# Both ends of an attention stage in new orders, and one turned tile in another PSUM bank

## The chip, the cores and the metric

The kernel runs on one core of one Trainium2 chip. The metric is the device time of one execution in microseconds (us); less is better.

A core has TensorE (PE, matrix products out of SBUF into the accumulators, PSUM), VectorE (DVE), ScalarE (ACT), GpSimd (POOL) and SyncE (SP, which here only issues transfers). Each engine runs its own instructions in the order in which the program lists them, and an instruction that has to wait for another engine holds up all that stand behind it on its own.

## The reference, cut to what matters

A macaron layer: half a feed-forward part, an attention part, half a feed-forward part, each added to its input. Tokens are 1024, channels C = 256, heads 16 of 16 channels, the inner width of the feed-forward part 768.

```python
x = x + 0.5 * ffn(layernorm(x))
x = x + attn(layernorm(x))
x = x + 0.5 * ffn(layernorm(x))

def attn(x):
    q, k, v = split(x @ w_qkv)
    q, k = xpos(q), xpos(k)
    scores = (q @ k.T) * D ** -0.5 * decay_mask
    y = scores @ v
    yn = (y - mean(y)) / sqrt(var(y) + eps)
    yn = yn * gn_weight + gn_bias
    return (silu(x @ w_g) * yn) @ w_proj

def ffn(x):
    return ((silu(x @ Wg * gs) * (x @ Wu * us)) @ Wd) * ds
```

The mean and variance in attn are over the 16 channels of a head. The score mask is causal and decays by a factor of the head for each step of distance.

## The kernel before, in words

**Tiles and stages.** The tokens are cut in NT = 8 tiles (in attention: chunks) of 128. The first feed-forward part works on two groups of four tiles: products gate and up in transposed form (gate_up, line 1148), then down (line 1171), which makes one token tile from 12 products of 128x128 by 128x256: six parts of the inner width, each in a high and a low half. `down(d, first, last)` does the parts from first to last, so a call can be cut in two. Attention runs chunk by chunk as a linear recurrence: a state of 16x16 per head is carried from chunk to chunk, and within a chunk the masked scores are multiplied out. The second feed-forward part follows as the first.

**One chunk c of attention.** PE turns the normalized tile (turn_h2, line 1201), ACT copies it (copy_h2, 465), PE makes q and k (project_qk, 1214), v (project_v, 1226) and the gate (project_g, 1239). DVE rotates q and k in two steps: rotate_parts (779, two products with the rotation table, out of the PSUM bank) and rotate (792, a difference and a sum). PE turns the result (turn_qk, 1254) and makes the scores (1265), DVE masks them in four instructions (mask_scores, 804). y is the sum of state times q (apply_state, 1285) and masked scores times v (values, 1297), in the lower half of PSUM bank 0 (`b_y`); the upper half holds the gate product (`b_g`). The state's new part is update_state (1312) on PE, mask_kv (812) on DVE, add_state (342) on POOL. ACT copies y out (copy_y), PE turns it back to tokens by channels (turn_y, 1323), ACT squares it (gsq) and copies it (gd) in take_y (520), DVE sums the squares per head (group_var, 838), POOL forms (sum/16 + eps) to the power -1/2 (group_roots, 332: a short instruction and the power on line 340), DVE multiplies (group_norm, 844, tile gn), PE turns it again (turn_gn, 1340), ACT applies weight and bias (affine, 530), DVE multiplies by the gate (gated, 852), PE multiplies by w_proj (project_out, 1353), and DVE adds it to the residual (add_proj, 859).

**The norm of a tile.** DVE makes mean and variance (tile_stats, 697, and mean_var, 707), POOL the root (roots, 312: lines 316 and 318), DVE the normalized tile (norm_tile, 718). Tiles are numbered through: 0 to 7 in the first part, 8 to 15 in attention, 16 to 23 in the second. Tiles 16 to 19 are turned by turn_h(2) (1101), eight transposes, and split by ACT and PE for the second feed-forward part.

**What sets the order.** Everything is ordered by hand: for each engine the calls are written out one after the other (POOL from line 350, ACT from 541, DVE from 864, PE from 1364), and each operation waits for counts of semaphores named after what has been done. On DVE the middle chunks are a loop (973 to 987), in front of it stand the instructions of chunks 0 and 1, behind it chunks 5 to 7 by hand. On PE the loop is on lines 1439 to 1452, the front of attention on 1405 to 1438, the back on 1453 to 1483. POOL's back is on lines 385 to 394.

**The banks.** `b_turned_y` and `b_gn` say in which PSUM bank the turned y and the turned gn (and behind it the output product) of each chunk lie: bank 7 for chunks 0 to 6 of the one and 0 to 5 of the other, lower half for y, upper half for gn. turn_y therefore waits for the readers of that bank:

```python
if c == 0:
    pe.wait_ge(yd_done, NT)
elif c == NT - 1:
    pe.wait_ge(sc_masked, HG * NT)
else:
    pe.wait_ge(gd_done, c)
```

Of the kernel before, what the change touches and what calls it, by code (L numbers as in the profile page):

```python
# [32 lines left out]
T, C, I = 1024, 256, 768  # L33
# [94 lines left out]
def macaron(nc, x, w_qkv, w_g, w_proj, gn_w, gn_b, gate_w, up_w, down_w, gate_s, up_s, down_s,  # L128
            rotation_t, mask_t, out):
    with ExitStack() as ctx:  # L130
# [86 lines left out]
        b_v, b_kv = bank[2][:, 0:C], bank[2][:, C:C + KC * 2 * D]  # L217
        b_sc = bank[3:7]
        b_qkT, b_turn = b_sc[0], b_sc[1]
        b_turned_y = [bank[7]] * (NT - 1) + [bank[5]]  # L220
        b_gn = [bank[7]] * (NT - 2) + [bank[6], bank[0]]


# [80 lines left out]
        @block.gpsimd  # L304
        def _(pool):
            def subtract(q):

                pool.wait_ge(added, q + 1)
                pool.tensor_tensor(packed(grid, q), piece(raws[PIECES[q][0]], q), packed(grid, q),  # L309
                                   ALU.subtract).then_inc(sub_pool, 1)  # L310

            def roots(i):

                a, b = root_groups[i]
                pool.wait_ge(aggr_done, b)
                pool.tensor_scalar(ve[:, a:b], mv[:, a:b, 1], EPS, None, ALU.add).then_inc(ve_done, 1)  # L316
                pool.wait_ge(ve_done, i + 1)
                pool.tensor_tensor(rstd[:, a:b], ve[:, a:b], neg_half[:, 0:b - a], ALU.pow).then_inc(rstd_done, 1)  # L318

            def rest_f(j):  # L320

                pool.wait_ge(fhi_done, j + 1)
                g, i = PRODUCTS[j]
                pool.tensor_tensor(flo[:, g % NG, i, :], fuse[:, j % FUSE_SLOTS, :], fhi[:, g % NG, i, :].bitcast(F32),
                                   ALU.subtract).then_inc(flo_pool, 1)

            def add_down(t):

                pool.wait_ge(yd_done, t + 1)
                pool.tensor_tensor(x1[:, t, :], yd[:, t % 2, :], xt[:, t, :], ALU.add).then_inc(x1_done, 1)  # L330

            def group_roots(c):
                pool.wait_ge(gvar_done, c + 1)
                if c >= 1:
                    pool.wait_ge(grstd_done, c)
                pool.tensor_scalar(gve[:, :], gvar[:, :], 1.0 / D, EPS, ALU.mult, ALU.add).then_inc(gve_done, 1)
                pool.wait_ge(gve_done, c + 1)
                if c >= 2:
                    pool.wait_ge(gn_done, c - 1)
                pool.tensor_tensor(grstd[:, c % 2], gve[:, :], neg_half[:, :], ALU.pow).then_inc(grstd_done, 1)  # L340

            def add_state(c):
                pool.wait_ge(kvm_done, c + 1)
                if c >= 2:
                    pool.wait_ge(state_done, c - 1)
                    pool.wait_ge(gn_done, c - 1)
                pool.wait_ge(y_done, c)
                pool.tensor_tensor(state[:, (c + 1) % 2], state[:, c % 2], kvm[:, :, :], ALU.add).then_inc(state_done, 1)

            pool.memset(neg_half[:, :], -0.5).then_inc(const_done, 1)  # L350
            pool.memset(v2[:, :, :, :, :], 0.0).then_inc(v_zero, 1)
            pool.wait_ge(const_done, 1)
            roots(0)
            roots(1)
            subtract(1)
            subtract(2)
            roots(2)
            subtract(4)
            subtract(5)
            rest_f(3)  # L360
            subtract(6)
            rest_f(4)
            subtract(7)
            rest_f(9)
            add_down(0)
            add_down(1)
            roots(X_ROOTS)
            roots(X_ROOTS + 1)
            rest_f(10)
            add_down(2)  # L370
            add_down(3)
            roots(X_ROOTS + 2)
            roots(X_ROOTS + 3)
            add_down(4)
            add_down(5)
            add_down(6)
            add_down(7)
            roots(X_ROOTS + 4)
            add_state(1)
            group_roots(0)  # L380
            for c in range(2, 5):
                roots(X_ROOTS + c + 3)
                group_roots(c - 1)
                add_state(c)
            group_roots(4)
            add_state(5)
            roots(X_ROOTS + 8)
            group_roots(5)
            roots(X_ROOTS + 9)
            add_state(6)  # L390
            group_roots(NT - 2)
            group_roots(NT - 1)
            roots(X_ROOTS + NT + 2)
            roots(X_ROOTS + NT + 3)

        @block.scalar
        def _(act):
# [122 lines left out]
            def take_y(c):  # L520

                act.wait_ge(y_turned, c + 1)
                if c >= 1:
                    act.wait_ge(gvar_done, c)
                nc.scalar.activation(gsq[:, :], b_turned_y[c][:, 0:C], ACT.Square).then_inc(gsq_done, 1)
                if c >= 2:
                    act.wait_ge(gn_done, c - 1)
                nc.scalar.activation(gd[:, c % 2], b_turned_y[c][:, 0:C], ACT.Copy).then_inc(gd_done, 1)

            def affine(c):  # L530

# [132 lines left out]
        def _(dve):  # L664
# [194 lines left out]
            def add_proj(c):  # L859
                dve.wait_ge(proj_done, c + 1)  # L860
                dve.tensor_tensor(x1[:, c, :], b_gn[c][:, C:2 * C], x1[:, c, :], ALU.add).then_inc(x2_done, 1)
# [104 lines left out]
            mask_scores(1, 3)  # L966
            tile_stats(12)
            mean_var(12)
            rotate_parts(3)
            mask_kv(1)  # L970
            norm_tile(12)
            group_var(0)
            for c in range(2, 5):
                mask_scores(c, 0)
                mask_scores(c, 1)
                rotate(c + 1)
                group_norm(c - 2)
                mask_scores(c, 2)
                if c >= 3:
                    add_proj(c - 3)  # L980
                mask_scores(c, 3)
                group_var(c - 1)
                norm_stats(NT + c + 3, NT + c + 4)
                gated(c - 2)
                rotate_parts(c + 2)
                mask_kv(c)
                norm_tile(NT + c + 3)
# [19 lines left out]
            rotate(7)  # L1007
            group_norm(4)
            mask_scores(6, 2)
            add_proj(3)  # L1010
            mask_scores(6, 3)
            group_var(5)
            tile_stats(19)
            norm_tile(16)
            mean_var(19)
            gated(4)
            norm_tile(17)
            norm_tile(18)
            mask_kv(6)
            norm_tile(19)  # L1020

            c, j0 = NT - 1, NG * NI
            mask_scores(c, 0)
            mask_scores(c, 1)
            group_norm(c - 2)
            mask_scores(c, 2)
            add_proj(c - 3)
            mask_scores(c, 3)
            group_var(c - 1)
            tile_stats(2 * NT + 4)  # L1030
            mean_var(2 * NT + 4)
# [63 lines left out]
        def _(pe):  # L1095
# [189 lines left out]
            def apply_state(c):  # L1285

                pe.wait_ge(yT_done, c)
                pe.wait_ge(sg_done, min(c + 2, NT))
                pe.wait_ge(qT_copied, c + 1)
                pe.wait_ge(kvm_done, 1)  # L1290
                if c >= 2:
                    pe.wait_ge(state_done, c - 1)
                for k in range(KC):
                    pe.matmul(b_y[:, k * P:(k + 1) * P], state[:, c % 2, k, :], qT[:, c % 2, k, :], start=(k == 0), stop=False,  # L1294
                              skip_group_check=True)
# [27 lines left out]
            def turn_y(c):  # L1323
                pe.wait_ge(yT_done, c + 1)

                if c == 0:
                    pe.wait_ge(yd_done, NT)
                elif c == NT - 1:
                    pe.wait_ge(sc_masked, HG * NT)
                else:  # L1330
                    pe.wait_ge(gd_done, c)
                    if c >= 2:
                        pe.wait_ge(ga_done, c - 1)
                    if c >= 3:
                        pe.wait_ge(x2_done, c - 2)
                for k in range(KC):
                    mm = pe.transpose(b_turned_y[c][:, k * P:(k + 1) * P], yT[:, c % 2, k, :], ident)
                mm.then_inc(y_turned, 1)

            def turn_gn(c):  # L1340
# [4 lines left out]
                    pe.wait_ge(sc_masked, HG * NT)  # L1345
                elif c >= 1:
                    pe.wait_ge(x2_done, c)
                pe.wait_ge(gd_done, min(c + 2, NT - 1))
                for k in range(KC):
                    mm = pe.transpose(b_gn[c][:, C + k * P:C + (k + 1) * P], gn[:, k * P:(k + 1) * P], ident)  # L1350
                mm.then_inc(gn_turned, 1)
# [1 line left out]
            def project_out(c):  # L1353
                pe.wait_ge(go_done, c + 1)
                if c == 0:
                    pe.wait_ge(wp_in, 16)
                pe.wait_ge(gd_done, min(c + 3, NT - 1))
                pe.wait_ge(ga_done, c + 1)
                for k in range(KC):
                    mm = pe.matmul(b_gn[c][:, C:2 * C], go[:, k, :], wp[:, k, :], start=(k == 0), stop=(k == KC - 1))  # L1360
# [60 lines left out]


            turn_qk(1)
            project_qk(2)
            values(0)
            update_state(0)
            scores(1)
            project_v(2)
            down(7)
            project_g(2)  # L1430
            turn_qk(2)
            turn_h2(3)
# [22 lines left out]
            project_g(7)  # L1455
            project_out(3)
            turn_qk(7)
            turn_gn(4)
            apply_state(6)
            values(6)  # L1460
            update_state(6)
            scores(7)

            c, j0 = NT - 1, NG * NI
# [73 lines left out]
```

## Time and profile before

| what | us |
|---|---|
| median of 3 runs | 159.44 |
| lowest and highest | 159.43 and 160.87 |
| the profiled execution, its own time | 159.59 |
| its span, first to last instruction | 157.8 |

The profile is of one execution. Times in it count from the start of the span, in us. A row of a timeline has the start, the busy time, the engine, the line of the kernel, the operation, the tile written and the tiles read, the shapes, how many instructions of that kind follow each other (x4), and in brackets how long the engine sat idle before and for whom it then went on. Neighbouring instructions of one engine overlap a little, so starts are better sums than durations. The chain of waits follows the work that ended last back to what released it; its pieces have a start and a length. In the rows a tile's name has no number: h on line 723 is a normalized tile, h on line 471 is h2.

### The profile page before, as it was taken

To read this page: it belongs to the slowest core of one execution; us is meant where nothing else is said; L and a number is where in the kernel's file an instruction comes from. 1 tells how busy PE (TensorE), PEld (TensorE's weight loads), DVE (VectorE), ACT (ScalarE), POOL (GpSimd) and SP (SyncE) were. 2 spreads that over 40 slices of the span, in tenths; PEclk is the share of its full clock that TensorE was granted. 3 is DMA by queue.
4 is the path that set the end of the run, shared out by engine and by line. 5 is a ranking of instruction groups with operands and counts; after the bars stand their busy time and mean duration, and the time that the engine had idled before them with its cause. 6 is when DMAs were issued, how large, how long until landed. Compare 5 with 4: busy or idle time off the path is not lost.

```text
span 157.8 us, 3711 instructions
## 1 busy us (share of the span) xinstructions
PE 147.1 (93%) x1327; PEld 117.2 (74%) x1327; DVE 121.6 (77%) x271; ACT 85.2 (54%) x203; POOL 68.3 (43%) x76
## 2 busy tenths in 40 slices
PE   5798999999999999995999999999599999999992
PEld 2275688788979659854796969698478888888991
DVE  0897999998897747464988888888564999656784
ACT  3476996786116073606565656566376557473310
POOL 3455444775963300318475747665659320000000
PEclk9999999999999999999999999999999999999999
DMA  4998404703000000000000000000000000001114
GB/s 139 317 369 301 164 0 127 278 2 133 0 0 4 0 0 4 0 4 0 0 6 0 6 0 6 0 4 0 0 6 0 0 4 0 0 0 58 42 36 135
DMA packets 7009, 8.47 MB, mean 54 GB/s; under 512 B 448, under 2 KB 5712, under 8 KB 6992
## 3 DMA queue, kind: packets, MB, share of 16 engines
q1 hardware_dynamic: 6816, 8.16, 15.3%
q8 instruction: 11, 0.18, 0.5%
q10 hardware_dynamic: 176, 0.07, 0.3%
q14 instruction: 6, 0.05, 0.1%
HBM read 7.19 MB, written 1.05 MB: 52 GB/s over the span
## 4 chain that ended last, share of the span: by engine, by line
PE 73%; POOL 9%; DVE 7%; issue 5%; ACT 2%; DMA 2%; ACTq 0%; POOLq 0%; DVEq 0%
PE bank L1167 26%; PE bank L1195 13%; PE bank L1223 9%; PE bank L1360 4%; POOL grstd L340 4%; PE bank L1236 4%; PE bank L1280 3%; PE bank L1307 3%; PE bank L1250 3%; POOL rstd L318 3%; DMA xt<-in_L_attn_x 2%; DVE stats L705 1%; PE bank L1294 1%; PE bank L1350 1%; PE bank L1262 1%
## 5 line engine op out<-in xcount | busy, mean ns | idle before, releaser
L1167 PE MATMUL bank<-hh,up_r 128*128 128x512 f32 x92 | 25.5, 400 | 0.1
L1167 PE MATMUL bank<-hh,gate_r 128*128 128x512 f32 x92 | 25.6, 401 | 0.0
L1195 PE MATMUL bank<-down_r,fhi 128*128 128x256 f32 x96 | 24.2, 290 | 0.0
L340 POOL TENSOR_TENSOR grstd<-gve,neg_half 128x16 f32<-128x16 f32 x8 | 23.4, 2925 | 0.7
L1195 PE MATMUL bank<-down_r,flo 128*128 128x256 f32 x96 | 23.4, 282 | 0.0
L455 ACT ACTIVATE gact<-bank,vec 128x512 f32<-128x512 f32 x24 | 16.3, 685 | 9.0 <-PE bank L1167 8.0
L463 ACT ACTIVATE fhi<-fuse 128x512 fp32r<-128x512 f32 x24 | 14.6, 625 | 10.8 <-DVE fuse L752 10.8
L1167 PEld LDWEIGHTS bank<-hh,up_r 128*128 128x128 f32 x92 | 16.8, 188 | 4.3 <-issue 0.6
L1167 PEld LDWEIGHTS bank<-hh,gate_r 128*128 128x128 f32 x92 | 16.9, 188 | 4.0 <-ACT gate_r L404 0.4
L1195 PEld LDWEIGHTS bank<-down_r,fhi 128*128 128x128 f32 x96 | 18.1, 188 | 0.7 <-issue 0.2
L1195 PEld LDWEIGHTS bank<-down_r,flo 128*128 128x128 f32 x96 | 18.1, 188 | 0.6 <-issue 0.2
L809 DVE TENSOR_TENSOR sc<-bank,msk 128x384 f32<-128x384 f32 x32 | 16.6, 549 | 1.9 <-PE bank L1280 1.9
L752 DVE SCALAR_TENSOR_TENSOR fuse<-bank,vec,gact 128x512 f32<-128x512 f32 x24 | 17.6, 743 | 0.2
L760 DVE TENSOR_TENSOR flo<-fuse,fhi 128x512 fp32r<-128x512 f32 x20 | 14.2, 728 | 3.1 <-ACT fhi L463 3.0
L1223 PE MATMUL bank<-wqkv,h 128*128 128x512 f32 x32 | 15.3, 599 | 0.3 <-ACT h L471 0.3
L309 POOL TENSOR_TENSOR grid<-raw,grid 128x768 f32<-128x768 f32 (+2 forms) x6 | 10.7, 1781 | 9.9 <-DVE raw L682 9.9
L316 POOL TENSOR_SCALAR ve<-mv 128x1 f32<-128x1 f32 (+3 forms) x15 | 4.6, 304 | 20.2 <-DVE mv L709 20.1
L789 DVE TENSOR_TENSOR rc<-bank,raw 128x512 f32<-128x512 f32 x8 | 5.5, 691 | 7.9 <-PE bank L1223 7.7
L330 POOL TENSOR_TENSOR x<-yd,xt 128x256 f32<-128x256 f32 x8 | 6.3, 801 | 11.9 <-DVE yd L772 11.9
L318 POOL TENSOR_TENSOR rstd<-ve,neg_half 128x1 f32<-128x1 f32 (+3 forms) x15 | 10.3, 687 | 1.3
L772 DVE TENSOR_TENSOR yd<-bank,ds 128x256 f32<-128x256 f32 x16 | 6.6, 420 | 5.0 <-PE bank L1195 5.0
L723 DVE TENSOR_SCALAR h<-x,mv,rstd 128x256 f32<-128x256 f32 x16 | 7.1, 457 | 3.1 <-POOL rstd L318 3.1
(90 smaller groups left out, 286.0 us busy)
## 6 DMA issues: line engine op xcount, KB each, us to landing
raw<-in_rotation SPq DMA_DIRECT2D x1, 1536.0 KB, 7.2
out<-xt SPq DMA_DIRECT2D x8, 128.0 KB, 1.7
raw<-in_L_ffn_down_w SPq DMA_DIRECT2D x2, 384.0 KB, 7.1
wqkv<-in_L_attn_w_qkv SPq DMA_DIRECT2D x1, 768.0 KB, 9.5
xt<-in_L_attn_x SPq DMA_DIRECT2D x2, 256.0 KB, 3.5
xt<-in_L_attn_x SPq DMA_DIRECT2D x1, 512.0 KB, 5.1
raw<-in_rotation SPq DMA_DIRECT2D x1, 512.0 KB, 3.2
raw<-in_L_ffn_gate_w SPq DMA_DIRECT2D x1, 384.0 KB, 5.7
```

The lines of the kernel that those rows point to most:

```text
L309: pool.tensor_tensor(packed(grid, q), piece(raws[PIECES[q][0]], q), packed(grid, q), ALU.subtract).then_inc(sub_pool, 1)
L318: pool.tensor_tensor(rstd[:, a:b], ve[:, a:b], neg_half[:, 0:b - a], ALU.pow).then_inc(rstd_done, 1)
L340: pool.tensor_tensor(grstd[:, c % 2], gve[:, :], neg_half[:, :], ALU.pow).then_inc(grstd_done, 1)
L455: nc.scalar.activation(gact[:, j % 2, :], pairs[j // (NG * NI)][j % 2][0][:, :], ACT.Silu, scale=gate_col[:, i:i + 1]).then_inc(silu_done, 1)
L463: nc.scalar.activation(fhi[:, g % NG, i, :], fuse[:, j % FUSE_SLOTS, :], ACT.Copy).then_inc(fhi_done, 1)
L723: dve.tensor_scalar(h[:, n % TH, :], src[:, n % NT, :], mv[:, n, 0:1], rstd[:, n:n + 1], ALU.subtract, ALU.mult).then_inc(h_done, 1)
L752: dve.scalar_tensor_tensor(out=fuse[:, j % FUSE_SLOTS, :], in0=pairs[j // (NG * NI)][j % 2][1][:, :], scalar=up_col[:, i:i + 1], in1=gact[ ...
L760: dve.tensor_tensor(flo[:, g % NG, i, :], fuse[:, j % FUSE_SLOTS, :], fhi[:, g % NG, i, :].bitcast(F32), ALU.subtract).then_inc(flo_dve, 1)
L809: dve.tensor_tensor(sc[:, r], b_sc[r][:, 0:KC * SP].rearrange("p (k t) -> p k t", t=SP), causal.unsqueeze(1).to_broadcast([P, KC, SP]), AL ...
L1167: mm = pe.matmul(dst[:, :], wr[m][:, k * I + i * P:k * I + (i + 1) * P], half[:, k, g % NG, :], start=(k == 0 and half is hhi), stop=(k == ...
L1195: mm = pe.matmul(downs[d][:, 0:C], half[:, g % NG, i, t * P:(t + 1) * P], wr["down"][:, i * C:(i + 1) * C], start=(i == 0 and half is fhi) ...
L1223: mm = pe.matmul(b_qk[:, :], h2[:, c % 2, k, :], wqkv[:, k, 0:2 * C], start=(k == 0), stop=(k == KC - 1))
```

## The change

It changes no operation, only where operations stand, one bank, and the waits that go with it.

- PE, front: the first half of down(7) goes ahead of project_qk(2), the second half stays.
- DVE, front: mask_kv(1), norm_tile(12) and group_var(0) go ahead of rotate_parts(3).
- POOL, back: the root of tile 19 (`X_ROOTS + 9`) and add_state(6) go ahead of group_roots(5).
- DVE, back: group_var(5) goes ahead of add_proj(3), mask_kv(6) ahead of the norms of 17 and 18, gated(4) behind them; in chunk 7 the four score masks stand together, and add_proj(4) comes ahead of group_norm(5).
- PE, back: apply_state(6) and update_state(6) go ahead of turn_gn(4).
- The turned y of chunk 6 goes to the upper half of bank 0. Its turn waits for the last gate instead of bank 7's readers, apply_state(7) waits for its copy gd(6), and the later users of bank 7 no longer do.

```diff
-        b_turned_y = [bank[7]] * (NT - 1) + [bank[5]]
+        b_turned_y = [bank[7][:, 0:C]] * (NT - 2) + [bank[0][:, C:2 * C], bank[5][:, 0:C]]
...
             roots(X_ROOTS + 8)
-            group_roots(5)
             roots(X_ROOTS + 9)
             add_state(6)
+            group_roots(5)
             group_roots(NT - 2)
...
-                nc.scalar.activation(gsq[:, :], b_turned_y[c][:, 0:C], ACT.Square).then_inc(gsq_done, 1)
+                nc.scalar.activation(gsq[:, :], b_turned_y[c], ACT.Square).then_inc(gsq_done, 1)
...
-                nc.scalar.activation(gd[:, c % 2], b_turned_y[c][:, 0:C], ACT.Copy).then_inc(gd_done, 1)
+                nc.scalar.activation(gd[:, c % 2], b_turned_y[c], ACT.Copy).then_inc(gd_done, 1)
...
             mean_var(12)
-            rotate_parts(3)
             mask_kv(1)
             norm_tile(12)
             group_var(0)
+            rotate_parts(3)
             for c in range(2, 5):
...
             mask_scores(6, 2)
+            group_var(5)
             add_proj(3)
             mask_scores(6, 3)
-            group_var(5)
             tile_stats(19)
             norm_tile(16)
             mean_var(19)
-            gated(4)
+            mask_kv(6)
             norm_tile(17)
             norm_tile(18)
-            mask_kv(6)
+            gated(4)
             norm_tile(19)
...
             mask_scores(c, 1)
+            mask_scores(c, 2)
+            mask_scores(c, 3)
+            add_proj(c - 3)
             group_norm(c - 2)
-            mask_scores(c, 2)
-            add_proj(c - 3)
-            mask_scores(c, 3)
             group_var(c - 1)
...
                     pe.wait_ge(state_done, c - 1)
+                if c == NT - 1:
+                    pe.wait_ge(gd_done, NT - 1)
...
                     pe.wait_ge(sc_masked, HG * NT)
+                elif c == NT - 2:
+                    pe.wait_ge(sg_done, NT)
                 else:
                     pe.wait_ge(gd_done, c)
...
-                pe.wait_ge(gd_done, min(c + 2, NT - 1))
+                pe.wait_ge(gd_done, NT - 1 if c == NT - 1 else min(c + 2, NT - 2))
...
-                pe.wait_ge(gd_done, min(c + 3, NT - 1))
+                pe.wait_ge(gd_done, min(c + 3, NT - 2))
...
             turn_qk(1)
+            down(7, 0, NI // 2)
             project_qk(2)
             values(0)
             update_state(0)
             scores(1)
             project_v(2)
-            down(7)
+            down(7, NI // 2)
             project_g(2)
...
             turn_qk(7)
+            apply_state(6)
+            update_state(6)
             turn_gn(4)
-            apply_state(6)
             values(6)
-            update_state(6)
             scores(7)
```

## Rows read from the trace of the kernel before

**Rows 1.** Busy time, share of the span and instructions of each engine.
```profile
PE 147.1 (93%) x1327; PEld 117.2 (74%) x1327; DVE 121.6 (77%) x271; ACT 85.2 (54%) x203; POOL 68.3 (43%) x76
```
**Rows 2.** Waits of PE, whole span: who for whom, us in total, times, longest.
```profile
PE bank L1350 <- DVE gn L849: 1.8, 1, 1.8
PE bank L1121 <- DVE h L723: 1.6, 1, 1.6
```
**Rows 3.** Chain of waits, down(7): start, length, piece.
```profile
62.09 1.42 PE bank L1195 x12
```
**Rows 4.** Timeline of PE, front of attention (start, us, engine, line, operation).
```profile
56.13 0.60 PE L1262 MATMUL bank<-msk,rot 128*128 128x128 f32 x4
57.07 1.98 PE L1223 MATMUL bank<-wqkv,h 128*128 128x512 f32 x4 [0.34 <-ACT h L471]
...
69.54 0.44 PE L1337 MATMUL bank<-msk,yT 128*128 128x128 f32 x2
70.36 1.10 PE L1236 MATMUL bank<-wqkv,h 128*128 128x256 f32 x4 [0.39 <-DVE kvm L819]
...
75.20 1.88 PE L1223 MATMUL bank<-wqkv,h 128*128 128x512 f32 x4
```
**Rows 5.** Timeline of DVE, front of attention.
```profile
65.27 0.18 DVE L709 BATCH_NORM_AGGREGATE mv<-stats 128x2 f32<-128x6 f32 x1
68.60 0.69 DVE L789 TENSOR_TENSOR rc<-bank,raw 128x512 f32<-128x512 f32 x1 [3.15 <-PE bank L1223]
...
70.14 0.40 DVE L723 TENSOR_SCALAR h<-x,mv,rstd 128x256 f32<-128x256 f32 x1
70.45 0.41 DVE L842 TENSOR_REDUCE gvar<-gsq 128x16 f32<-128x256 f32 x1
...
71.71 0.42 DVE L801 TENSOR_TENSOR rot<-rc,rs 128x256 f32<-128x256 f32 x1
```
**Rows 6.** Timeline of ACT, copy of h2 of chunk 4.
```profile
73.20 0.38 ACT L471 ACTIVATE h<-bank 128x256 f32<-128x256 f32 x1
```
**Rows 7.** Timeline of POOL, both ends of attention.
```profile
65.85 0.57 POOL L318 TENSOR_TENSOR rstd<-ve,neg_half 128x1 f32<-128x1 f32 x1
70.30 0.83 POOL L348 TENSOR_TENSOR state<-state,kvm 128x256 f32<-128x256 f32 x1 [3.88 <-DVE kvm L819]
...
71.50 2.92 POOL L340 TENSOR_TENSOR grstd<-gve,neg_half 128x16 f32<-128x16 f32 x1
...
112.29 0.72 POOL L348 TENSOR_TENSOR state<-state,kvm 128x256 f32<-128x256 f32 x1
...
116.39 2.92 POOL L340 TENSOR_TENSOR grstd<-gve,neg_half 128x16 f32<-128x16 f32 x1
...
119.92 2.90 POOL L340 TENSOR_TENSOR grstd<-gve,neg_half 128x16 f32<-128x16 f32 x1
```
**Rows 8.** Timeline of PE, back of attention.
```profile
110.19 0.44 PE L1337 MATMUL bank<-msk,yT 128*128 128x128 f32 x2
110.79 0.85 PE L1121 MATMUL bank<-msk,h 128*128 128x128 f32 x6 [0.16 <-issue]
113.22 0.44 PE L1121 MATMUL bank<-msk,h 128*128 128x128 f32 x2 [1.59 <-DVE h L723]
...
125.69 1.03 PE L1360 MATMUL bank<-wp,go 128*128 128x256 f32 x4
```
**Rows 9.** Timeline of DVE, back of attention.
```profile
106.85 0.43 DVE L861 TENSOR_TENSOR x<-bank,x 128x256 f32<-128x256 f32 x1 [0.47 <-PE bank L1360]
...
108.63 0.17 DVE L709 BATCH_NORM_AGGREGATE mv<-stats 128x2 f32<-128x6 f32 x1
112.36 0.81 DVE L723 TENSOR_SCALAR h<-x,mv,rstd 128x256 f32<-128x256 f32 x1 [1.82 <-POOL rstd L318]
...
122.85 0.42 DVE L849 TENSOR_TENSOR gn<-gd,grstd 128x256 f32<-128x256 f32 x1
...
125.06 0.46 DVE L857 TENSOR_TENSOR go<-ga,sg 128x256 f32<-128x256 f32 x1
```

## The prediction

> **What bounds the kernel now.** I read the page's shares first: TensorE (PE) is busy for 93% of the span, VectorE (DVE), the next, for 77% [rows 1]. So the time is PE's own work plus the gaps in it, and an edit pays only where it closes a gap or makes one. Next the waits of PE over the whole span: of those behind the start only five are above 0.1 us, and all lie where the change is. The two long ones are 1.8 us for the first normalized group (gn) and 1.6 us for the normalized tile 19 [rows 2]. The others are best seen in brackets in the timeline of PE: 0.34 us before q and k of chunk 2, 0.39 us before v of chunk 3, 0.16 us before the turn of h for the second feed-forward part [rows 4, 8]. Their sum is 4.3 us; a gap also costs the refill of the pipeline behind it. Between the two ends of attention PE is gapless, so what is won at the front is carried to the back, as long as the engines that feed it move along.
>
> **Why the gaps are there.** Front: DVE ends its work on tile 12 at 65.45 and then sits 3.15 us, because the next instruction in its order is the rotation of chunk 3, which waits for q and k of chunk 3 [rows 5]. The state mask, the norm of tile 12 and the first group sum stand behind it though they don't need it; that sum comes at 70.45. ScalarE (ACT) may not square chunk 1 before it (line 524), and GpSimd (POOL) starts the state sum at 70.30 and the 2.92 us power only at 71.50 [rows 7]. PE's 0.39 us and 1.8 us are the tail of this. Back: POOL has the power of chunk 5 ahead of the root of tile 19, so tile 19 is normalized at 112.36, and PE's last pair of turns waits until 113.22 [rows 8, 9].
>
> **Part 1, half a down product ahead of q and k.** Twelve products of down(7) take 1.42 us [rows 3], so six take 0.71. turn_qk(1) ends at 56.13 + 0.60 = 56.73, so the half ends by 57.44, and project_qk(2) waited until 57.07 anyway [rows 4]. By ends of instructions it would be 0.37 late, and 0.34 of the 0.71 is won; but matmuls overlap their neighbours' tails and the first one after a gap pays a refill, so it may be all 0.71. I take 0.65 (q and k about 0.06 late), as the stalled q and k took 1.98 us and the unstalled one at 75.20 took 1.88 [rows 4]. What hides the half is the copy of h2(2) on ACT. The second half then ends 0.65 earlier, and so do scale_down(7), project_g(2) and all up to the scores of chunk 2.
>
> **Part 2, mask, norm and group sum ahead of the rotation.** DVE: nothing is added, four short instructions move into its 3.15 us of idle time. Shifted by 0.65, mv(12) starts at 64.62 and the root (0.58 later, 0.57 long [rows 5, 7]) ends at 65.77. The norm of tile 12 then runs beside POOL's state sum. A norm beside a state sum took 0.81 instead of 0.40 at 112.3 [rows 5, 7, 9], so I count 0.8: norm until 66.6, group sum (0.41) until 66.95. POOL: the state sum is long done, and the power starts some 0.4 behind the group sum (one short instruction and two hand-overs; an estimate from 70.45 + 0.41 to 71.50, where the state sum stood between [rows 5, 7]), at 67.35; with 2.92 it ends at 70.27. DVE meanwhile does rotate_parts(3) when q and k(3) are there (68.60 - 0.65 = 67.95), two score masks and rotate(3). Of the 3.11 us from 68.60 to 71.71 mask, norm and group sum took about 1.0 (three of some 0.33 start to start [rows 5]), so rotate(3) starts near 70.05 and, with two halves of 0.42, ends near 70.8. group_norm(0) finds its power done and is finished near 71.2. PE: turn_y(1) at 69.54 - 0.65 = 68.89; project_v(3) without its 0.39 us at 69.16 to 69.33, 1.10 long [rows 4]. What is late next is ACT: h2(4) ended 2.12 us after project_v(3) did (73.58 against 71.46 [rows 4, 6]), which gives 72.4 to 72.55. PE would be ready at 71.9 to 72.4 (75.20 less 0.65, 0.39, 1.8 and up to 0.5 of refills). So project_qk(4) starts at 72.4 to 72.6 instead of 75.20 [rows 4]: 2.6 to 2.8 for both parts together. I take 2.7; a gap of up to 0.5 us stays there, with ACT's h2 as releaser.
>
> The norm beside the state sum is where a rule of the Trainium skill is to be weighed (SBUF — State Buffer, section "Who interferes with whom"): DVE and GpSimd share a port pair, held for a whole instruction, and a DVE instruction in a two-port mode or with two SBUF inputs contends with a GpSimd one that reads SBUF. The 0.81 us agrees. But half of a rotation, both inputs in SBUF, took its usual 0.42 us at 71.71, in the middle of the power that ran from 71.50 [rows 5, 7]; for the power the rule does not hold. If it did, at the back gated(5) would wait out the power of chunk 6 (below, until 117.60), the group sum of 7 behind it would end near 118.4, and the last power would start some 0.6 us later: 155.6 instead of 155.0.
>
> **Part 3, the back end.** Times are those of before; all shift by 2.7. DVE does group_var(5) in the 0.47 us in which it waited for project_out(3), so mv(19) comes about 0.33 earlier than 108.63, at 108.30 [rows 9]. On POOL the root of 19 is now next: it ends 1.15 later (0.58 + 0.57, as for tile 12 [rows 5, 7]), near 109.45. On DVE mask_kv(6), two norms and gated(4) lie in between, so tile 19 is normalized at 109.7 to 110.5, the last figure with the state sum beside it. PE: turn_gn(4) waits for add_proj(3), which ends at 106.85 + 0.43 [rows 9]; apply_state(6) and update_state(6) now go in front of it, so that PE loses nothing there. turn_y(6), at 110.19 before, comes up to 0.3 earlier (my estimate of that wait), turn_h(2) at about 110.15, without its 0.16; six of its turns took 0.85, so its last pair is at 110.8 instead of 113.22 [rows 8]: 2.4 us, or 2.1 if the 0.3 isn't there. The new wait of apply_state(7) for gd(6) holds up values(7) and everything behind it; gd(6) is done a turn of 0.44 and two ACT instructions of 0.38 after turn_y(6) starts [rows 6, 8], near 111.1, while PE gets to apply_state(7) near 111.9, behind that last pair and project_out(4) (1.03, as in 125.69). I count nothing; without that cover it is 0.8 at most, and leaving bank 7 takes waits away rather than adding any.
>
> What is late next is POOL. Its chain: root of 19 to 109.45, state sum of 6, and power of 5 at 110.62 (1.20 behind the state sum, as 70.30 to 71.50 [rows 7]) until 113.54. Then gn(5), sum of 6 on DVE and power of 6: 1.14 from end to start (0.03 as from the last power's end at 122.82 to 122.85, 0.33 for gn start to start, 0.41 for the sum and 0.37 until the power, as in the front [rows 5, 7, 9]), so from 114.68 to 117.60. The last power starts 0.61 behind that (116.39 + 2.92 to 119.92 [rows 7]) and ends at 121.11. gn(7) at 121.14, gated(7) 2.21 later as in 122.85 to 125.06, project_out(7) 0.63 behind that [rows 8, 9]: 123.98 at the latest, 123.85 if the 0.63 held some queueing. Before it was 125.69 [rows 8]. So of PE's 2.4 us only 1.7 to 1.85 stays; I take 1.8. Everything behind project_out(7) is gapless and moves along.
>
> **Sum.** 2.7 + 1.8 = 4.5 us. The profiled execution took 159.59 (span 157.8 and 1.79 around it), 0.15 above the median of 159.44. 159.59 - 4.5 = 155.1; from the median 154.9. I forecast 155.0, 2.8% less; its own range is 154.2 to 155.7 (front 2.3 with the small end of part 1, to 2.8; end 1.4 to 2.4). A measurement can tell about 1% from no change.
>
> **Rivals.**
> *The back doesn't pay (0.15).* The powers fall behind so far that they eat the 2.4 us; then 159.44 - 2.7 = 156.7. For it: three powers now stand behind the root and the state sum, with next to no idle POOL time between. Against: the chain above is made of rows that repeat to 0.1 us.
> *PE alone decides (0.12).* POOL's chain and ACT's h2 are quicker than I read them: 3.1 (project_qk(4) at 72.1, the middle of 71.9 to 72.4) + 2.4 = 5.5, so 153.9. For it: PE's gaps sum to 4.3 before refills. Against: the h2 and gn rows.
> *The front doesn't pay (0.07).* A wait that I overlooked holds DVE, for one mask_kv(1), ahead of the rotation: only the back pays, 159.44 - 1.8 = 157.6. Against: DVE idles 3.15 us there.
> *Slower (0.04).* POOL's order. The powers of 5, 6 and 7 now wait, in order, for mask_kv(6) and the state sum of 6, which wait for update_state(6). Each us by which that sum comes after 109.4 reaches project_out(7) in full; 1.8 late eats the back, 4.5 late eats all, so it decides against the change from a state sum at 113.9. Held until tile 19's mask queue of chunk 7, say 6.5 late, the time is 161.4. Against: the product has only the turned q and k and gate_silu(7) before it, both there by 107.
> The rest (0.62) is the forecast. That the change doesn't do what it says is the first and the third of them.
>
> **How the numbers follow.** Forecast and PE-alone lie within 153.7 to 155.7 (0.2 us of reading error below 153.9); to hold 8 in 10 the range takes in the back rival with 0.3 for its own error: 153.7 to 157.0. Faster by over 1% (below 157.85): all but the slower case and half of the front rival, cut a little for overlooked waits: 0.91. Within 1%: 0.05, slower 0.04.
>
> **What would show it.** Right: PE's waits no longer list gn(0) near 1.8 or tile 19; DVE's 3.15 us before rc are some 1 us; the first power starts near 67, not 71.5; project_qk(4) at 72.4 to 72.6 behind ACT's h2; turn_h(2) whole in one run; small PE gaps of 0.2 to 0.5 us before turn_gn(5) and turn_gn(7), released by gn; powers 5, 6 and 7 with about 1 us between them at most. Wrong: a gap before apply_state(7) behind gd; a late state sum of 6; a gap at project_qk(2) or values(0).

## The result and the profile after

The changed kernel takes 155.31 us (median of 4 executions, 155.17 to 155.35); the forecast was 155.0, the range 153.7 to 157.0. Its ratio to the kernel before is 0.9686, with a 95% interval of 0.9609 to 0.9764; against the 159.44 of before it is 0.974. The profiled execution took 155.30 with a span of 153.5, so 4.29 us less than the 159.59 of before. (The median of before was 160.16 beside these runs and not 159.44: two of its four executions took 160.87 and 161.50, as long as those in which TensorE's granted clock was seen to fall for a while, see the last section.)

PE's waits in the changed kernel (who for whom, us in total, times, longest). The 1.8 and the 1.6 of [rows 2] are gone, and what is left behind the start is 0.8 us in three gaps.

```profile
PE bank L1354 <- DVE gn L849: 0.4, 2, 0.3
PE bank L1223 <- ACT h L471: 0.4, 1, 0.4
```

Front of attention, timelines of PE, DVE and POOL of the changed kernel (columns as in [rows 4, 5, 7]).

```profile
56.35 0.60 PE L1262 MATMUL bank<-msk,rot 128*128 128x128 f32 x4
...
57.51 1.88 PE L1223 MATMUL bank<-wqkv,h 128*128 128x512 f32 x4
59.31 0.87 PE L1309 MATMUL bank<-sc,v 128*32 128x128 f32 x32
...
69.15 0.44 PE L1341 MATMUL bank<-msk,yT 128*128 128x128 f32 x2
69.42 1.03 PE L1236 MATMUL bank<-wqkv,h 128*128 128x256 f32 x4
...
72.61 1.98 PE L1223 MATMUL bank<-wqkv,h 128*128 128x512 f32 x4 [0.40 <-ACT h L471]
74.43 0.61 PE L1296 MATMUL bank<-qT,state 128*128 128x128 f32 x4
```

```profile
66.05 0.41 DVE L723 TENSOR_SCALAR h<-x,mv,rstd 128x256 f32<-128x256 f32 x1
66.39 0.42 DVE L842 TENSOR_REDUCE gvar<-gsq 128x16 f32<-128x256 f32 x1
68.20 0.69 DVE L789 TENSOR_TENSOR rc<-bank,raw 128x512 f32<-128x512 f32 x1 [1.40 <-PE bank L1223]
...
71.00 0.42 DVE L849 TENSOR_TENSOR gn<-gd,grstd 128x256 f32<-128x256 f32 x1
```

```profile
66.16 0.89 POOL L348 TENSOR_TENSOR state<-state,kvm 128x256 f32<-128x256 f32 x1
67.13 0.20 POOL L336 TENSOR_SCALAR gve<-gvar 128x16 f32<-128x16 f32 x1
67.42 2.92 POOL L340 TENSOR_TENSOR grstd<-gve,neg_half 128x16 f32<-128x16 f32 x1
```

In DVE's rows the group sum stands at 66.39 instead of 70.45, in POOL's the first power at 67.42 instead of 71.50, and v of chunk 3 (69.42) has lost its wait. q and k of chunk 4 start at 72.61 instead of 75.20; the bracket names ACT's copy of h2.

Back of attention, PE, then DVE and POOL of the changed kernel.

```profile
107.93 1.04 PE L1121 MATMUL bank<-msk,h 128*128 128x128 f32 x8
108.80 1.03 PE L1364 MATMUL bank<-wp,go 128*128 128x256 f32 x4
109.67 0.61 PE L1296 MATMUL bank<-qT,state 128*128 128x128 f32 x4
...
111.70 0.44 PE L1354 MATMUL bank<-msk,gn 128*128 128x128 f32 x2 [0.16 <-DVE gn L849]
...
119.27 0.44 PE L1354 MATMUL bank<-msk,gn 128*128 128x128 f32 x2 [0.25 <-DVE gn L849]
...
121.34 1.04 PE L1364 MATMUL bank<-wp,go 128*128 128x256 f32 x4
```

```profile
107.23 0.82 DVE L723 TENSOR_SCALAR h<-x,mv,rstd 128x256 f32<-128x256 f32 x1
...
118.78 0.43 DVE L849 TENSOR_TENSOR gn<-gd,grstd 128x256 f32<-128x256 f32 x1 [0.73 <-POOL grstd L340]
```

```profile
107.06 0.84 POOL L348 TENSOR_TENSOR state<-state,kvm 128x256 f32<-128x256 f32 x1
...
108.27 2.92 POOL L340 TENSOR_TENSOR grstd<-gve,neg_half 128x16 f32<-128x16 f32 x1
...
115.85 2.90 POOL L340 TENSOR_TENSOR grstd<-gve,neg_half 128x16 f32<-128x16 f32 x1
```

The eight turns of turn_h(2) are one row without a wait, where [rows 8] has six and, 1.59 us later, two. Two small gaps have come instead, before turn_gn(5) at 111.70 and turn_gn(7) at 119.27; DVE's gn(7) waited 0.73 us for POOL's power, which is the chain the prediction named.

Whole times mix these gains with the start: before the change's place is reached, kernels that are alike up to there differ by up to 0.7 us (turn_qk(1) begins at 55.85 in one profile, at 56.53 in another). So the experiments are read by two stretches of PE's timeline: the front, from the start of turn_qk(1) to the start of the state product of chunk 2 (in the changed kernel 74.43 - 56.35 = 18.08), and the back, from there to project_out(7) (121.34 - 74.43 = 46.91).

| kernel | front, us | back, us | median, us |
|---|---|---|---|
| before | 20.79 | 48.77 | 159.44 |
| changed | 18.08 | 46.91 | 155.31 |
| e11, changed again | 18.09 | 46.91 | 155.20 |
| e1, down(7) whole behind v | 18.70 | 46.92 | 155.45 |
| e12, the same again | 18.71 | 46.91 | 155.82 |
| e10, down(7) whole ahead of q and k | 18.49 | 46.86 | 155.57 |
| e2, rotation of chunk 3 first | 20.18 | 46.84 | 157.10 |
| e3, front only | 18.08 | 50.10 | 156.74 |
| e9, back only | 21.83 | 47.43 | 158.49 |
| e4, sixth y in bank 7 | 18.08 | 46.90 | 155.31 |
| e5, power of 5 first | 18.08 | 47.03 | 155.28 |
| e6, group sum of 5 early | 18.08 | 46.40 | 154.68 |
| e7, h2 ahead of the gate's silu | 17.80 | 46.92 | 154.89 |
| e8, both | 17.86 | 46.34 | 154.33 |

In the profile of e3 the clock fell in the back, in that of e9 from 74 to 82 us, in both stretches: these three figures are not for comparison. Nor is e9's median, which lies between two times of 157.57 and two of 159.4. In the kernel before, project_out(7) begins at 125.69 [rows 8] and the state product of chunk 2 here:

```profile
76.92 0.61 PE L1294 MATMUL bank<-qT,state 128*128 128x128 f32 x4
```

So the change won 2.71 us in the front and 1.86 in the back, 4.57 in all; 0.22 us of it went back into a later start of this profile and 0.06 into the stretch behind project_out(7).

### The profile page after: what moved, and what is told of

It reads as the page before. It is cut to its first block, busy times and chain, and to the rows that moved or that the text cites. A ratio compares the mean times of both kernels' runs of the same rounds, so it can differ in the third digit from the quotient of the medians.

```text
span 153.5 us, 3712 instructions
## 1 busy us (share of the span) xinstructions
PE 147.2 (96%) x1327; PEld 117.4 (76%) x1327; DVE 121.4 (79%) x271; ACT 85.2 (56%) x203; POOL 68.5 (45%) x76
## 4 chain that ended last, share of the span: by engine, by line
PE 74%; POOL 10%; DVE 6%; issue 4%; ACT 3%; DMA 2%; POOLq 0%; ACTq 0%; DVEq 0%
PE bank L1167 23%; PE bank L1195 14%; PE bank L1223 9%; POOL grstd L340 6%; PE bank L1280 5%; PE bank L1236 5%; PE bank L1250 4%; PE bank L1364 3%; PE bank L1309 3%; DMA xt<-in_L_attn_x 2%; POOL rstd L318 2%; PE bank L1262 2%; DVE stats L705 2%; PE bank L1296 1%; PE bank L1341 1%
## 5 line engine op out<-in xcount | busy, mean ns | idle before, releaser
L1280 PEld LDWEIGHTS bank<-qT,kM 32*128 32x128 f32 x256 | 7.9, 186 | 2.0 <-issue 1.5
```

The lines of the kernel that those rows point to most:

```text
L1280: mm = pe.matmul(b_sc[r][:, k * SP + half * P:k * SP + P + half * HP], kM[at, k, half].rearrange("p m s -> p (m s)"), qT[at, c % 2, k, hal ...
```

## The experiments

**The half down product.** e1 and e12 undo it:

```diff
-            down(7, 0, NI // 2)
             project_qk(2)
...
-            down(7, NI // 2)
+            down(7)
```

> The changed kernel (155.3 us) with part 1 undone: down(7) whole, behind v of chunk 2. My theory: the half product costs q and k of chunk 2 only about 0.1 us and takes 0.71 us out of the path behind them, so without it 155.9 (0.6 more). Rival: it only fills the 0.34 us that PE idled there, so 155.6.

Median 155.45, 0.14 above the changed kernel: by whole times the rival's 155.6 is nearer. But its front is 18.70, 0.62 longer. The profile also started earlier (turn_qk(1) at 55.95, not 56.35), so whole times and stretches disagreed, and both kernels ran again, side by side.

> The changed kernel once more, beside the next two. The times of whole executions differ by 0.2 to 0.5 us for something that lies before the change: the first tiles of x landed at 4.33 us in its profile and at 3.95 in that of the kernel with down(7) whole. My theory: that lies with the single execution or load and not with the kernel, so the first landing moves away from 4.33 and the time lies anywhere in 154.9 to 155.5. Rival: each program has its own start, so 4.3 and 155.3 again.

> The kernel with down(7) whole, behind v of chunk 2, once more. Counted from turn_qk(1) to the state product of chunk 2 it was 0.62 us longer than the changed kernel, by whole times only 0.15. My theory: the 0.62 stands in the stretch, and the whole time comes out 0.3 to 0.9 above the changed kernel's in the same call. Rival: the half product wins 0.15 and no more, 155.45 again.

155.20 and 155.82: 0.62 apart, and the stretches repeat to 0.01. The half product is worth 0.62. What moves the start isn't settled: the first tiles landed at 4.17 in e11 and at 4.33 in the first profile of the same kernel, less of a move than between some different kernels. The landing alone isn't it: in e4 and e8 they landed at 4.21 and 4.20, and turn_qk(1) began at 56.53 and 56.22.

e10 puts all of down(7) ahead of q and k:

> The changed kernel with all of down(7) ahead of q and k of chunk 2, so that these come about 0.7 us later than now. My theory: PE does the same work without a gap and q and k of chunk 2 have slack on DVE, so the stretch from turn_qk(1) to the state product of chunk 2 stays at 18.1 (18.0 to 18.3). Rival: q and k are on the path and all behind them is late by the other half, 18.8 and a time 0.7 longer.

Neither: 18.49, so 0.41 of the 0.71 is lost. The state product of chunk 1 and the copies on ACT show where, here in e10:

```profile
65.17 0.68 PE L1296 MATMUL bank<-qT,state 128*128 128x128 f32 x4 [0.17 <-issue]
```

```profile
63.55 1.11 ACT L485 ACTIVATE v<-bank 64x128 f32<-64x128 f32 x4
64.68 0.38 ACT L494 ACTIVATE sg<-bank 128x256 f32<-128x256 f32 x1
```

And here in the changed kernel:

```profile
64.72 0.61 PE L1296 MATMUL bank<-qT,state 128*128 128x128 f32 x4
64.04 0.38 ACT L494 ACTIVATE sg<-bank 128x256 f32<-128x256 f32 x1 [0.20 <-PE bank L1250]
```

v of chunk 2 comes later too, and the silu of its gate stands behind the copies of v on ACT; the state product of chunk 1, which waits for that silu (line 1288 of the kernel before), stalls where the half product let it through. Counted from turn_qk(1) it starts 0.34 us later (65.17 - 56.46 against 64.72 - 56.35), most of the 0.41. Half is the better of these cuts.

**The order on DVE in front.** e2:

```diff
+            rotate_parts(3)
             mask_kv(1)
             norm_tile(12)
             group_var(0)
-            rotate_parts(3)
```

> The changed kernel with part 2 undone: on DVE the rotation of chunk 3 again ahead of the state mask, the norm of tile 12 and the first group sum. My theory: the first power starts 4 us later, PE waits for gn(0) again, 157.4 (2.1 more). Rival: only PE's two gaps of before, 0.39 and 1.76, less the 0.40 that stands now, come back: 157.05.

The front grows by 2.10, within a hundredth of what 2.71 less the half product leaves. The median, 157.10, lies by the rival's figure; but the start of this profile was 0.23 early (56.12 against 56.35) and its back 0.07 shorter, and with both added the time is my 157.4. PE's waits of e2 have gn back (1.8 of the 2.2 is gn(0)), and v's:

```profile
PE bank L1354 <- DVE gn L849: 2.2, 3, 1.8
PE bank L1236 <- DVE kvm L819: 0.4, 1, 0.4
```

**Front and back alone.** e3 undoes the back whole, e9 the front whole.

> The changed kernel with all of the back undone (POOL, DVE and PE orders and the bank of the sixth turned y as before), the front as changed. My theory: front and back add up, 157.15 (1.85 more), with PE's gap before the turn of tile 19 back at 1.6. Rival: with the front 2.7 us earlier the old back loses less, 156.3.

> The kernel before with the back changed alone, the front as before. My theory: 158.0 (2.7 more than the changed kernel), and with the run that has the front alone the two gains sum to the whole of 4.3 to 4.5. Rival: the back only pays behind a faster front, 159 or more.

e3's front is 18.08, that of the changed kernel. Its executions without a fall of the clock took 156.65 to 156.76: above the rival's 156.3, and 0.4 to 0.5 under my 157.15; its profile starts 0.5 earlier than the changed kernel's (55.85 against 56.35), which would account for that if those executions started as early; no trace here shows it. PE's wait for tile 19 is back, 1.59 us. e9 took 157.57 in two executions and 159.4 in two. The 157.57 is 1.87 below the 159.44 of before, the back's 1.86, and 1.8 to 2.2 below the executions of before beside it at full clock (159.33 to 159.73). So the two ends add up as far as whole times tell; in the executions of 159.4 the clock fell (last section).

**The bank.** e4 undoes `b_turned_y` and the waits that go with it.

> The changed kernel (155.3 us) with the turned y of chunk 6 back in bank 7 and the waits that belong to that, all orders as changed. My theory: the move of the bank costs and gains nothing, as every reader that the old waits name is done in time: 155.3, within 0.1. Rival: it is the move that lets project_out(4) and turn_gn(5) go on without gd(6): 155.7 or more.

155.31 and both stretches the same: in these orders the move of the bank is worth nothing, and its new wait costs nothing.

**POOL's order.** e5:

```diff
+            group_roots(5)
             roots(X_ROOTS + 9)
             add_state(6)
-            group_roots(5)
```

> The changed kernel with only POOL's order undone: the power of chunk 5 again ahead of the root of tile 19 and the state sum of 6. My theory: its sum now comes some 3 us earlier than before, so the power is over near 107.5, tile 19 is late by 0.5 to 0.9 and not by 1.6, and gn(5) is no longer late: 155.6 (0.3 more, 0.2 to 0.6). Rival: POOL's order is the whole of the back's gain, 157.0 or more.

155.28, under the 155.6 that I expected and far from the rival's 157.0, and a back only 0.12 longer. A wait for tile 19 is there again, but of 0.5, and none for gn:

```profile
PE bank L1121 <- DVE h L723: 0.5, 1, 0.5
PE bank L1223 <- ACT h L471: 0.4, 1, 0.4
```

So the swap on POOL, which looks like the point of the back, trades one late thing for another. It isn't needed once DVE hands POOL the sum of chunk 5 early. In the kernel before that sum (L842) and its power are here:

```profile
107.65 0.41 DVE L842 TENSOR_REDUCE gvar<-gsq 128x16 f32<-128x256 f32 x1
108.44 3.03 POOL L340 TENSOR_TENSOR grstd<-gve,neg_half 128x16 f32<-128x16 f32 x1
```

In e5 they are here, with the root of tile 19 and its turns:

```profile
103.56 0.41 DVE L842 TENSOR_REDUCE gvar<-gsq 128x16 f32<-128x256 f32 x1
104.34 2.90 POOL L340 TENSOR_TENSOR grstd<-gve,neg_half 128x16 f32<-128x16 f32 x1
107.52 0.58 POOL L318 TENSOR_TENSOR rstd<-ve,neg_half 128x1 f32<-128x1 f32 x1
109.00 0.44 PE L1121 MATMUL bank<-msk,h 128*128 128x128 f32 x2 [0.54 <-DVE h L723]
```

Counted from the state product of chunk 2 (76.92 and 74.15), the sum begins 1.32 us earlier than before, the power 1.33, and PE's last pair of turns (before at 113.22) 1.45, of the 1.74 that e5's back wins. That is read from the chain; no run moves the sum alone, so how the 1.74 divides among it and the other moves of the back is not shown.

**What still holds the kernel.** e6 puts the group sum of 5 ahead of rotate(7), so that its power falls into the 3.14 us that POOL idles before the root of 19, and in chunk 7 it puts gn(5) and the sum of 6 ahead of add_proj(4); e7 swaps two calls on ACT in chunk 2 of the loop; e8 has both.

```diff
             mask_scores(6, 1)
+            group_var(5)
             rotate(7)
             group_norm(4)
             mask_scores(6, 2)
-            group_var(5)
...
             mask_scores(c, 3)
-            add_proj(c - 3)
             group_norm(c - 2)
             group_var(c - 1)
+            add_proj(c - 3)
...
+            group_roots(5)
             roots(X_ROOTS + 9)
             add_state(6)
-            group_roots(5)
...
                 copy_v(c + 1)
-                gate_silu(c + 1)
-                copy_h2(c + 2)
+                if c == 2:
+                    copy_h2(c + 2)
+                    gate_silu(c + 1)
+                else:
+                    gate_silu(c + 1)
+                    copy_h2(c + 2)
```

> A new order of the back: on DVE the group sum of chunk 5 ahead of the rotation of chunk 7, on POOL its power in the 3 us that POOL idles before the root of tile 19, and gn(5) and the sum of 6 ahead of add_proj(4). My theory: POOL's chain of powers is what holds the back now, so PE's gaps before turn_gn(5) and turn_gn(7) (0.16 and 0.25 and their refills) go: 154.7 (0.5 to 0.7 less). Rival: those gaps are put down to gn but something else (ACT, gated) is as late: 155.2 or more.

> The changed kernel with one swap on ACT: in chunk 2 of the loop the copy of h2(4) goes ahead of the silu of the gate. My theory: what holds q and k of chunk 4 is that copy alone, so they start 0.28 earlier: 155.0. Rival: the silu is then late for the state product of chunk 2, or the gap is refill: 155.3.

> The early group sum of chunk 5 and the swap on ACT together. My theory: the one lies in the back and the other in the front, so they add up: 0.28 + 0.51 = 0.8 less than the changed kernel by stretches, 154.3 to 154.6. Rival: behind a faster front the back's chain on POOL binds again, 154.7.

The power of chunk 5 in e6, and the idle time of POOL in the changed kernel that it goes into:

```profile
103.57 3.11 POOL L340 TENSOR_TENSOR grstd<-gve,neg_half 128x16 f32<-128x16 f32 x1
```

```profile
106.11 0.22 POOL L316 TENSOR_SCALAR ve<-mv 128x1 f32<-128x1 f32 x1 [3.14 <-DVE mv L709]
```

e6: back 46.40 (0.51 less), 154.68. Both gn waits are gone from PE's list, so POOL's chain of powers, and the sums on DVE that feed it, were what held the back. e7: front 17.80 (0.28 less), 154.89; PE's wait for ACT's copy of h2 is gone, so that copy was what held q and k of chunk 4. e8: 154.33, a ratio of 0.961 (0.9567 to 0.9652) to the kernel before and 0.87 below the changed kernel's 155.20 beside it; by stretches 0.22 + 0.57 = 0.79. It is faster than both kernels, and of the 5.36 us that its two stretches win over the kernel before, 0.79 is beyond the change. Between turn_qk(1) and the end its PE has no wait in the list.

## Why the prediction was right, and where its terms were off

It came out at 155.3 for 155.0, with the gains where it put them.

- **Part 1, 0.65.** Measured 0.62 (e12). The reading that starts and ends of matmuls overlap, so that the half costs q and k little, holds: values(0) starts 2.96 behind turn_qk(1), where it was 2.86 (56.13 to 58.99), 0.10 late instead of 0.06. The two durations that the 0.06 was read from don't carry it: q and k of chunk 3 took 1.98 us as well and waited for nothing (66.18 in the changed kernel). From its start to that of values(0), q and k took 1.92 with the wait (57.07 to 58.99) and 1.80 without (57.51 to 59.31).
- **Part 2, 2.05 of the 2.7.** Measured 2.10 (e2). ACT's h2 as what is late next, and a gap of up to 0.5 us with that releaser, were right: 0.40, and e7 removes it. One term was wrong without harm: the norm of tile 12 took 0.41 and not 0.81, as it began 0.1 us ahead of the state sum, and it was POOL's sum that took 0.89. It ended at 67.05, behind the group sum (66.81) and not long before it, and the power began 0.37 later. The "four short instructions" are three: one each for the mask, the norm and the sum. gn(0) was done at 71.42, near the forecast 71.2, the start being 0.22 later.
- **Part 3, 1.8.** Measured 1.86. Put at the changed kernel's times (2.7 earlier, 0.22 later for the start), POOL's chain came out as summed: the power of 5 at 108.27 for 108.14, gn(7) at 118.78 for 118.66, project_out(7) at 121.34 for 121.37 to 121.50. PE alone was to win 2.4; e6, where gn no longer waits, wins 2.37, so the difference is POOL's powers and the sums that feed them. What was off is the reason given: the root of tile 19 "now next" on POOL was taken as what makes the back pay. e5 has the old order on POOL and loses 0.12 of 1.86. The early group sum on DVE was counted only as 0.33 us of tile 19's statistics, and not as a power 1.3 us earlier, which e5's rows show.
- **The bank.** Counted at nothing; e4 gives nothing. PE reached apply_state(7) at 109.67, and gd(6) was done 0.88 before (108.41 + 0.38 on ACT's timeline).
- **The rivals.** e2, e3 and e9 rule out that one end doesn't pay. That PE alone decides is out by the two waits that stood as forecast, for ACT's h2 and for gn; with both gone (e8) the stretches win 5.36, near the 5.5 of that rival. The slower case needed a state sum of 6 by 4.5 us late: reckoned at 109.45 less 2.7 and with a start 0.22 later, so at 106.97, it began at 107.06.
- **Norm and state sum.** Where the two met, the one that began later took longer: DVE's norm 0.82 us at 107.23, instead of 0.40, beside the sum of 107.06; POOL's sum 0.89 at 66.16, instead of 0.72, beside the norm of 66.05. The Trainium skill (SBUF — State Buffer, section "Who interferes with whom") says that whichever of the two issues first holds the shared port pair; the traces agree on which one pays. For the power the prediction took no such wait, and there was none: gated(5) took 0.42 us inside the power of chunk 6, so the 155.6 that such a wait would have given is out.

```profile
112.35 2.90 POOL L340 TENSOR_TENSOR grstd<-gve,neg_half 128x16 f32<-128x16 f32 x1
```

```profile
113.02 0.42 DVE L857 TENSOR_TENSOR go<-ga,sg 128x256 f32<-128x256 f32 x1 [0.49 <-ACT ga L536]
```

- **The total.** 2.71 + 1.86 = 4.57 against 4.5. The time is 0.3 above the forecast since the start was later by 0.22, the end took 0.06 longer, and the forecast lay 0.1 below 159.59 - 4.5, halfway to the median.

## What to carry to other kernels

When an engine executes in order, an instruction that waits long should have everything that doesn't need it in front of it: here three short instructions moved into a 3.15 us wait on VectorE were worth 2.1 us on TensorE. Before a fix of the engine that is late is believed, ask when it was handed its work: without the swap on GpSimd the back lost 0.12 of its 1.86 us, as VectorE's sum came 1.3 us earlier there too. Where whole times move by half a microsecond at the start, compare a stretch between two fixed instructions; in the two kernels that ran twice it repeated to 0.01 us.

## What the runs showed of the hardware that was not expected

A long wait of TensorE can cost more than itself. In e9, whose front is that of the kernel before, the wait for gn(0) was 1.75 us; then the granted clock fell. PE's timeline of e9, and busy times by stretch (from and to, length, then PE, PEld, DVE, ACT and POOL busy with the number of instructions, the granted clock as a share of 2.4 GHz, DMA share and GB/s):

```profile
74.86 0.44 PE L1354 MATMUL bank<-msk,gn 128*128 128x128 f32 x2 [1.75 <-DVE gn L849]
75.13 2.96 PE L1223 MATMUL bank<-wqkv,h 128*128 128x512 f32 x4
77.89 1.06 PE L1296 MATMUL bank<-qT,state 128*128 128x128 f32 x4
```

```profile
70.00:74.00 4.00, 2.81 (x18) 2.31 (x18) 2.40 (x7) 2.56 (x9) 3.60 (x3) 1.00 0.00 0
74.00:78.00 4.00, 3.14 (x7) 1.44 (x8) 2.52 (x7) 1.81 (x5) 1.43 (x4) 0.72 0.00 0
78.00:82.00 4.00, 4.00 (x91) 3.54 (x90) 2.90 (x6) 0.94 (x3) 3.60 (x2) 0.85 0.02 6
82.00:86.00 4.00, 4.00 (x25) 3.12 (x24) 3.45 (x11) 3.18 (x11) 0.08 (x1) 1.00 0.00 0
```

The same q and k took 2.96 us where [rows 4] have 1.88 behind a wait of the same length, and the means of 0.72 and 0.85 are stretches partly at the lower level, 1.2 GHz. e3 shows the like behind its 1.59 us wait for tile 19: project_out(4) took 1.92 us instead of 1.03, and the mean clock from 110 to 114 us was 0.57.

```profile
110.27 0.53 PE L1121 MATMUL bank<-msk,h 128*128 128x128 f32 x2 [1.59 <-DVE h L723]
110.59 1.92 PE L1360 MATMUL bank<-wp,go 128*128 128x256 f32 x4
```

It does not come in every execution: of 29 of the kernel before beside the experiments, 12 had a mean clock of 1.000 and took 159.3 to 159.9, and 17 one of 0.986 or 0.989 and took 160.6 to 161.9. With one of the two long waits left it came in 2 of 4 (e9), 1 of 4 (e3) and 0 of 4 (e2, whose wait for gn(0) was 1.8 us). The 10 executions of the changed kernel had 0.997 to 1.000, and so had the 44 of the other kernels without either wait. The Trainium skill (TensorE: Matmul & The Clock Gate, section "Part 1: The HAM clock gate") says that idleness of the engine lets its clock fall to half; the traces agree in kind. With the two long waits gone the change won, besides its 4.3 us, what the clock cost the kernel before in more than half of its executions, 1.2 to 2.2 us against the median of those at 1.000 beside them; no term of the prediction had that. Why the clock falls in some executions and not in others is open. It does not account for every long execution: one of e11 took 156.43 at 0.997, and what held it is open too.
